# Mixture-of-experts stage of a two-layer transformer: from one tile per pipeline step to two

## The reference, cut to what matters

```python
z_norm = _rmsnorm(z, norm_w)
scores = softmax(z_norm @ router_w)                  # 8 experts
topk_vals, topk_idx = top_k(scores, 2)               # then divided by their sum
mixed = sum_e cw[:, e] * ((silu(z_norm @ w1[e]) * (z_norm @ w3[e])) @ w2[e])   # 128 -> 256 -> 128
z = z + mixed
```

## Time and profile before

| | us |
|---|---|
| median of 3 runs | 2763.26 |
| lowest, highest | 2757.63, 2775.57 |
| the profiled execution, its own time | 2753.16 |
| its span in the profile | 2751.4 |
| mean granted clock of TensorE over the span | 0.888 |
| expert tiles, first to last input transpose | 1600.8 to 2690.2 |

### The profile page before, as it was taken

The page is one execution under the profiler, slowest core; times in us unless marked ns, Lnnn a source line. Parts: engine busy times, 40 slices in busy tenths (PEclk is TensorE's granted clock), DMA queues, the critical chain, the costliest instruction groups (busy, mean ns, idle before and its releaser), DMA issues. The chain is left out here.

```text
span 2751.4 us, 46785 instructions
## 1 busy us (share of the span) xinstructions
PE 2116.8 (77%) x14679; PEld 1042.8 (38%) x14679; DVE 1843.9 (67%) x5385; ACT 1460.1 (53%) x3354; POOL 1225.6 (45%) x1710
## 2 busy tenths in 40 slices
PE   5999999999899899999999455674838575666762
PEld 1222222222256444444444234452526353444441
DVE  8999999999867788888888454453534344344324
ACT  1888888888833477777777322241414232333231
POOL 5433434342002477777775244335352524433434
PEclk9999999999999799999999777686968787777886
DMA  6535444353101233233332112222222222222322
GB/s 162 135 99 147 114 121 127 112 142 106 56 1 46 48 94 95 72 72 95 94 84 59 52 59 68 59 68 61 75 62 67 68 66 66 71 65 62 90 77 83
DMA packets 224609, 226.92 MB, mean 82 GB/s; under 512 B 34032, under 2 KB 187504, under 8 KB 224368
## 3 DMA queue, kind: packets, MB, share of 16 engines
q1 hardware_dynamic: 152432, 164.62, 22.5%
q0 software_dynamic: 16384, 33.59, 4.2%
q10 hardware_dynamic: 55552, 25.71, 3.2%
HBM read 96.48 MB, written 125.76 MB: 81 GB/s over the span
## 5 line engine op out<-in xcount | busy, mean ns | idle before, releaser
L702 ACT ACTIVATE mid_PT<-mid_ps 128x512 f32<-128x512 f32 (+2 forms) x1792 | 913.9, 568 | 258.2 <-PE mid_ps L583 250.3
L785 DVE TENSOR_REDUCE mid_nmax<-mid_ps 128x1 f32<-128x512 f32 (+2 forms) x1280 | 777.0, 658 | 61.7 <-PE mid_ps L562 36.8
L562 PE MATMUL mid_ps<-KT,QT 48*128 48x512 bf16 (+3 forms) x2048 | 605.0, 351 | 68.2 <-DVE mid_nmax L785 49.7
L1379 PE MATMUL moe_ps<-moe_w,moe_xinT 128*128 x638 | 398.4, 711 | 309.8 <-ACT moe_xinT L1434 159.0
L583 PE MATMUL mid_ps<-QT,KT 64*128 64x512 bf16 (+3 forms) x2048 | 562.5, 346 | 2.6 <-ACT mid_PT L702 2.2
L1528 DVE TENSOR_TENSOR moe_h<-moe_ps,moe_sg 128x256 f32<-128x256 f32 x319 | 135.1, 423 | 528.1 <-ACT moe_sg L1443 331.8
L599 PE MATMUL mid_ps<-mid_PT,vv 128*32 128x512 f32 (+3 forms) x4096 | 464.9, 527 | 16.2 <-POOL mid_PT L914 12.4
L1434 ACT ACTIVATE moe_xinT<-moe_ps,norm_w 128x128 f32<-128x128 f32 x319 | 117.0, 367 | 652.1 <-remote 349.7
L1490 POOL DMA_INDIRECT rows_in<-moe_xn,moe_scat_idx x256 | 248.4, 970 | 453.9 <-DVE moe_scat_idx L1676 380.1
L562 PEld LDWEIGHTS mid_ps<-KT,QT 48*128 48x128 bf16 x2048 | 159.0, 94 | 585.8 <-DVE mid_nmax L785 397.7
L1503 POOL DMA_INDIRECT moe_yg<-rows_out,moe_gat_idx x256 | 246.1, 961 | 241.3 <-issue 121.5
(11 more groups left out here) (260 smaller groups left out, 3028.3 us busy)
## 6 DMA issues: line engine op xcount, KB each, us to landing
l_spread<-mid_slots SPq DMA_DIRECT2D x128, 384.0 KB, 5.4
rows_in<-mid_blank SPq DMA_DIRECT2D x64, 512.0 KB, 3.7
QT<-l_spread SPq DMA_DIRECT2D x128, 192.0 KB, 4.4
KT<-l_spread SPq DMA_DIRECT2D x128, 192.0 KB, 5.2
moe_xin<-rows_in SPq DMA_DIRECT2D x319, 64.0 KB
rows_out<-moe_y ACTq DMA_DIRECT2D x319, 64.0 KB
x<-in_L_attn_x_dram SPq DMA_DIRECT2D x8, 512.0 KB, 6.3
QT<-mid_mrows SPq DMA_DIRECT2D x256, 6.0 KB
```

Of the source, the lines that this page charges most:

```text
L562: mm = pe.matmul(ps[:, bank, n_keys * a:n_keys * (a + 1)], QT[rows, par, pair, i * P:(i + 1) * P], KT[rows, par, pair, 0:n_keys], start=Tr ...
L702: act.activation(weights_of(r, i, heads), ps[:, ring(S2, n - 2, k), 0:widths[i] * len(heads)], ACT.Exp, scale=scale).then_inc(exp_done, 1)
L785: dve.tensor_reduce(to, of, X_AXIS, ALU.max, negate=True).then_inc(s1_used, 1)
L1379: mm = pe.matmul(ps[:, GU[v % BANKS], :], xinT[:, v % 2, :], w13[:, bass.ds(expert(v), 1), :].rearrange("p a f -> p (a f)"), start=True, s ...
```

## The change

Tiles go in pairs through the same pipeline. A unit gets one tile more, so that its count is even. TensorE does each of its four kinds of work for the two tiles of a pair and signals once; ScalarE copies both inputs in one instruction (128x256), both transposed h in one (128x512) and does one silu for both (128x512 from two banks); VectorE has one product and one copy per pair, and one store carries both results. Ages are now 2, 4 and 6 pairs. The ring is 4 pairs. PSUM: two pairs of banks for gate/up, one bank for the transposed h of a pair, two banks that each hold a pair's inputs and results, and one bank for the side transposes, the router and the counts together. So there are new waits: the h transposes wait for the copy of the pair before (`h_copied`), the side transposes for the last step of the group before (`scat_ready`), the result copy for the input copy out of the same bank (`x_copied`). The order on TensorE in a step is now: result, gate/up, h, input. Side steps run behind pairs, TensorE's one pair later, and `begin` and `transfers` are written anew.

```diff
-    RING, HELD = 8, 8
-    TURN, MULT, LAG = 6, 2, 8
-    BANKS = 3
+    RING, HELD = 4, 12
+    MULT, TURN, LAG = 2, 4, 6
...
-    tiles_in = [2 * IT * n + EXPERTS - 1 for n in sizes]
+    tiles_in = [2 * IT * n + EXPERTS for n in sizes]
     base_of = [sum(tiles_in[:u]) for u in range(UNITS + 1)]
     N = base_of[UNITS]
+    PAIRS = N // 2
...
-    begin = {2: 0, 3: 14, 4: 29, 5: 47, 6: 63, 7: 78, 8: 95, 9: 115, 10: 135, 11: 157, 12: 179, 13: 201, 14: 223, 15: 246,
-             16: 270, 17: 283, 18: 292, 19: 314, 20: 325}
-    transfers = ("s0 s1 s2 s3 g8 s4 s5 g9 s6 g10 s7 g11 s8 g12 s9 g13 s10 g14 s11 s12 g15 s13 g16 s14 g17 g18 s15 "
+    begin = {2: 0, 3: 15, 4: 31, 5: 49, 6: 63, 7: 81, 8: 97, 9: 120, 10: 141, 11: 163, 12: 183, 13: 205, 14: 225, 15: 251,
+             16: 281, 17: 301, 18: 309, 19: 319, 20: 333}
+    transfers = ("s0 s1 s2 s3 s4 g8 s5 g9 s6 s7 g10 g11 s8 s9 g12 s10 g13 g14 s11 s12 g15 g16 s13 s14 g17 g18 s15 "
                  "g19 g20 g21 g22 g23").split()
...
 
-        return 16 * sum(1 for n in range(base_of[u + 1]) if n % RING == s)
+        return 16 * sum(1 for p in range(base_of[u + 1] // 2) if p % RING == s)
...
-        GU, XHY, T, R = (0, 1, 2), (3, 4, 5), 6, 7
-        X, H, Y = 0, P, P + FF
-        psR = ps[:, R, 0:IT * EXPERTS].rearrange("p (t e) -> p t e", e=EXPERTS)
-        psK = ps[:, R, IT * EXPERTS:(2 * IT + 1) * EXPERTS].rearrange("p (t e) -> p t e", e=EXPERTS)
+        GU, H, XY, S = (0, 2), 4, (5, 6), 7
+        X, Y = 0, 2 * P
+        psR = ps[:, S, 0:IT * EXPERTS].rearrange("p (t e) -> p t e", e=EXPERTS)
+        psK = ps[:, S, IT * EXPERTS:(2 * IT + 1) * EXPERTS].rearrange("p (t e) -> p t e", e=EXPERTS)
...
+        xin = sb("xin", [P, RING, 2, DIM], F32)
+        xinT = sb("xinT", [P, 2, 2 * P], F32)
+        sg = sb("sg", [P, 2, 2, FF], F32)
+        h = sb("h", [P, 2, 2, FF], F32)
+        hT = sb("hT", [P, 2, 2 * FF], F32)
+        y = sb("y", [P, RING, 2, DIM], F32)
...
-        def run(tile, side, behind):
+        def run(duo, side, behind):
 
             for k in range(EARLY):
                 for s in range(STAGES):
                     side(k, s)
-            for n in range(N + LAG + 1 + behind):
-                tile(n)
-                for k, s in sides(n - behind):
-                    side(k, s)
+            for p in range(PAIRS + LAG + 1 + behind):
+                duo(p)
+                for n in range(2 * (p - behind), 2 * (p - behind) + 2):
+                    for k, s in sides(n):
+                        side(k, s)
...
-                row = sp.value_load(row_of[0:1, n:n + 1], min_val=0, max_val=EXPERTS * CAP - P)
-                if n >= RING:
-                    sp.wait_ge(step_done, n - RING + 1)
-                sp.dma_start(xin[:, n % RING, :], rows_in[u % CHUNKS][bass.ds(row, P), :]).then_inc(x_loaded[n % RING], 16)
+                for j in range(2):
+                    n = 2 * p + j
+                    row = sp.value_load(row_of[0:1, n:n + 1], min_val=0, max_val=EXPERTS * CAP - P)
+                    if j == 0 and p >= RING:
+                        sp.wait_ge(step_done, p - RING + 1)
+                    sp.dma_start(xin[:, p % RING, j, :], rows_in[u % CHUNKS][bass.ds(row, P), :])\
+                      .then_inc(x_loaded[p % RING], 16)
...
-            def tile(n):
-                if n == 0:
+            def duo(p):
...
+                bank = XY[p % 2]
+                if is_pair(p - 2):
+                    pe.wait_ge(x_copied, p - 1)
+                if is_pair(p - 2 - LAG):
+                    pe.wait_ge(y_ready, p - 2 - LAG + 1)
+                v = p - LAG
+                if is_pair(v):
+                    pe.wait_ge(h_copied, v + 1)
+                    for j in range(2):
+                        e = expert(2 * v + j)
+                        for c in range(FF // P):
+                            mm = pe.matmul(ps[:, bank, Y + j * DIM:Y + (j + 1) * DIM],
+                                           hT[:, v % 2, j * FF + c * P:j * FF + (c + 1) * P],
+                                           w2[:, bass.ds(e, 1), c, :].rearrange("p a d -> p (a d)"),
+                                           start=(c == 0), stop=(c == FF // P - 1))
+                v = p - MULT
+                if is_pair(v):
                     pe.wait_ge(x_copied, v + 1)
-                    if v >= BANKS:
-                        pe.wait_ge(h_ready, v - BANKS + 1)
-                    mm = pe.matmul(ps[:, GU[v % BANKS], :], xinT[:, v % 2, :],
-                                   w13[:, bass.ds(expert(v), 1), :].rearrange("p a f -> p (a f)"), start=True, stop=True)
-                v = n - LAG
-                if is_tile(v):
-                    e = expert(v)
-                    pe.wait_ge(h_copied, v + 1)
-                    for c in range(FF // P):
-                        mm = pe.matmul(ps[:, bank, Y:Y + DIM], hT[:, v % 2, c * P:(c + 1) * P],
-                                       w2[:, bass.ds(e, 1), c, :].rearrange("p a d -> p (a d)"),
-                                       start=(c == 0), stop=(c == FF // P - 1))
-                if is_tile(n):
-                    pe.wait_ge(x_loaded[n % RING], 16 * (n // RING + 1))
-                    mm = pe.transpose(ps[:, bank, X:X + P], xin[:, n % RING, :], w["ident"][:, :])
-                    pe.reg_load(held[n % HELD], expert_of[0:1, n:n + 1])
-                if n < N + LAG:
+                    if v >= 2:
+                        pe.wait_ge(h_ready, v - 1)
+                    for j in range(2):
+                        mm = pe.matmul(ps[:, GU[v % 2] + j, :], xinT[:, v % 2, j * P:(j + 1) * P],
+                                       w13[:, bass.ds(expert(2 * v + j), 1), :].rearrange("p a f -> p (a f)"),
+                                       start=True, stop=True)
+                v = p - TURN
+                if is_pair(v):
+                    pe.wait_ge(h_ready, v + 1)
+                    if v >= 1:
+                        pe.wait_ge(h_copied, v)
+                    for j in range(2):
+                        for c in range(FF // P):
+                            mm = pe.transpose(ps[:, H, j * FF + c * P:j * FF + (c + 1) * P],
+                                              h[:, v % 2, j, c * P:(c + 1) * P], w["ident"][:, :])
+                if is_pair(p):
+                    pe.wait_ge(x_loaded[p % RING], 32 * (p // RING + 1))
+                    for j in range(2):
+                        mm = pe.transpose(ps[:, bank, X + j * P:X + (j + 1) * P], xin[:, p % RING, j, :], w["ident"][:, :])
+                        pe.reg_load(held[(2 * p + j) % HELD], expert_of[0:1, 2 * p + j:2 * p + j + 1])
+                if p < PAIRS + LAG:
                     mm.then_inc(step_done, 1)
...
@@ -1402,15 +1415,15 @@
                         pe.wait_ge(added, k - GROUPS + 1)
                     else:
                         pe.wait_ge(z_ready, k + 1)
-                    if k + a >= 1:
-                        pe.wait_ge(t_used, 2 * k + a)
+                    if a == 1:
+                        pe.wait_ge(t_used, 2 * k + 1)
+                    elif k >= 1:
+                        pe.wait_ge(scat_ready, k)
                     for t in range(4):
-                        mm = pe.transpose(ps[:, T, t * P:(t + 1) * P], z[:, tiles_of(k) + 4 * a + t, :], w["ident"][:, :])
+                        mm = pe.transpose(ps[:, S, t * P:(t + 1) * P], z[:, tiles_of(k) + 4 * a + t, :], w["ident"][:, :])
                     mm.then_inc(t_made, 1)
                 if s == 8:
                     pe.wait_ge(t_used, 2 * k + 2)
-                    if k >= 1:
-                        pe.wait_ge(scat_ready, k)
...
-            run(tile, side, 2)
+            run(duo, side, 1)
...
+            def duo(p):
+                if p < PAIRS + LAG:
+                    act.wait_ge(step_done, p + 1)
+                if is_pair(p):
+                    act.activation(xinT[:, p % 2, :], ps[:, XY[p % 2], X:X + 2 * P], ACT.Copy, scale=w["norm_w"][:, 0:1])\
                        .then_inc(x_copied, 1)
-                v = n - TURN
-                if is_tile(v):
-                    act.activation(hT[:, v % 2, :], ps[:, XHY[n % BANKS], H:H + FF], ACT.Copy).then_inc(h_copied, 1)
-                v = n - MULT
-                if is_tile(v):
-                    if v >= BANKS:
-                        act.wait_ge(h_ready, v - BANKS + 1)
-                    act.activation(sg[:, v % BANKS, :], ps[:, GU[v % BANKS], 0:FF], ACT.Silu).then_inc(sg_ready, 1)
-                v = n - LAG - 1
-                if is_tile(v):
+                v = p - MULT
+                if is_pair(v):
+                    if v >= 2:
+                        act.wait_ge(h_ready, v - 1)
+                    act.activation(sg[:, v % 2, :, :], ps[:, GU[v % 2]:GU[v % 2] + 2, 0:FF], ACT.Silu).then_inc(sg_ready, 1)
+                v = p - TURN
+                if is_pair(v):
+                    act.activation(hT[:, v % 2, :], ps[:, H, :], ACT.Copy).then_inc(h_copied, 1)
```

(27 more changed lines are left out.)

45 lines of the change are left out of this document (10 added, 35 removed).

## The result

The pair kernel takes 2796.08 us (median of 4 runs, 2792.77 to 2798.28) beside 2760.45 for the one before (median of 4): ratio 1.0114, 95% interval [1.0092, 1.0135]. The forecast was 2713 us, faster; the measured value is the one of the rival in which a batch lets a fixed amount of work pass (2797), but the terms that make it up are largely others, as the last part shows. The profiled execution took 2795.2 us, span 2793.5, clock 0.884.

What follows compares the result with a forecast made beforehand. The prediction saw TensorE held by late signals during GpSimd's batches of indirect DMAs. Its terms, +21 - 80 + 13 - 4 = -50 us, took the 2763.3 us median to 2713 us; 8-in-10 range 2615 to 2790.

Steps and rivals of the forecast that it cites:

- a batch lets a fixed amount of work pass: Rival: windows over GpSimd's batches still pass 5 or 6 tiles, the change only adds tiles and waits: +34, 2797 us; chance 0.24.
- Item 1: Tiles: 8 spare tiles per unit instead of 7, nine more empty tiles at 2.33 us: +21 us (bounds 15 and 44).
- Item 2: In the batches: 1.5 more tiles pass per window, 23 windows at 2.33 us a tile: -80 us (bounds 0 and -204).
- Item 4: Places and waits: the single h bank's and VectorE's new waits stay hidden: 0 to +0.8 us a pair.
- the head start of 4 tiles: In a batch, TensorE gets 4 tiles instead of 2 beyond the last signal, less about one: +1 tile per window.
- a slow rhythm of 12.3 us per pair: In a stalled batch, a pair takes 12.3 us, 6.15 per tile instead of 7.8: +0.6 tile per window.
- Item 3: Instructions merged on ScalarE and VectorE: shorter per pair, but beside a busy TensorE, so 0 saved on the path.
- the two signs of being wrong: Signs of "wrong altogether": TensorE under 90% busy between batches, or batches moved so that more stand back to back.
- Item 5: Routing steps 5 and 6 fall into the same pair for 12 of 14 groups, 1.05 us each: +13 us (bounds 0, 36.4).
- The new starts and the new order at 0, with +-15.: Routing steps' new start numbers and the new order of transfers: put at 0, with +-15 us.
- Item 6: The tail behind the last input transpose: 6 pair drain steps instead of 8 steps: -4 us (bounds -10 and +5).

Runs made afterwards that it cites:

- a_gu_h2: Pair kernel with two banks for h, gate and up of both tiles sharing one bank (first tile computed with the second's): 2769.59 us, ratio 1.0019.

## Why the prediction was wrong

Where the time goes was seen rightly: into late signals in the batches, not into TensorE's own work. How many steps get through a batch was seen wrongly. Step by step:

**Item 1, +21.** 15.5 measured, within its bounds (15 and 44), the four batches that joined by it included.

**Item 2, -80: the step that failed.** "TensorE may still run two steps beyond the last signal, but a step is now two tiles". It may not. Item 4 looked at the single h bank only for the time between batches. The wait for `h_copied` of the pair before is a wait for the signal of the step before, and in a batch that is the late one. So the head start of 4 tiles was that of one pair and two thirds of the next, and a window passes 5.7 tiles, not 7.3. The second term of the item, a slow rhythm of 12.3 us per pair, failed as well: it was a line through two points, 7.79 us from one window and 5.3 from the drain, and the copies come 7 to 43 us apart. Put back, the second step ahead is worth 27.4 us, and not 80: with two h banks a window holds 7.1 tiles by its input transposes (135 in 19 windows; 113 with one bank), but only 0.6 tile more by its matmuls, and the joined batches have no second share. In the earlier trace rows the prediction read 41 as the lower end of the matmuls in a single batch; it is 33 (1644.1 to 1666.7).

"A batch lets a fixed amount of work pass" was given 0.24 and has come out in its main claim, that the change brings nothing per window, with two corrections: the amount is that of a window, however many batches it holds, and it does grow a little with the steps ahead. That its 2797 us is the measured time is luck: its +34 were 21 for tiles and 13 for side waits. Measured are 15.5 for the tiles, nothing for the side waits in this kernel, and about 14 for the order of the transfers, which it had at 0. Nor do the single changes add up: tiles 15.5, h bank 27.4 and order 14 make 57 where the pair kernel is 36 slower.

**Item 3, 0.** Right, and the sizes too: product 0.690 us (0.7 taken), ScalarE per pair 0.474 + 0.591 + 0.599 = 1.66 us (1.76 taken).

**Item 4, 0 to 0.8 us a pair.** Right between the batches (7.4 us in all where nothing is held), wrong in them, see item 2. Of the two signs of being wrong that the prediction named, one is batches that stand back to back more often, and these it got. The other, TensorE under 90% busy between batches (88%), is met only by the cut of the windows, as shown above.

**Item 5, +13.** In the pair kernel the idle time before the side transposes is unchanged (35.8). The collision is real, but hidden behind the h bank, and where a batch stands over it, it isn't 1.05 us but 14 (in a_gu_h2).

**"The new starts and the new order at 0, with +-15."** At the upper end: the order alone is 14 us, and 11 instead of 6 batches are joined, 9 with the old order. The prediction had counted 29 batches in 23 windows and then averaged over the windows, without asking what a joined batch costs more than a single one.

**Item 6, -4.** +15 by the profiled execution: g22 starts right behind g21, and under it the last pairs stand until 2740. But another execution of the same kernel parts loop and tail otherwise (a tail of 54.2 us, 7 less than before), so the size of this term stays open. Moving g22 away brings 5.6 us.

In what the forecast left out, a tile between batches takes 2.17 us instead of 2.30. With the batches apart pairs are 24 us faster than single tiles (2738.0 to 2714.08). No run tells what makes these 24 us.

## What to carry to other kernels

Before counting how many steps an engine may run ahead, follow every wait of the step back to the signal that it hangs on; one buffer that lost its twins shortens the whole pipeline, though its wait is hidden in the quiet stretches. Where a disturbance has a fixed price per stretch, look first at how many stretches there are and which join: 3.1 us of pause between two batches passed six tiles more, and keeping batches apart took 28 us off one kernel and 82 off the other, where the edits of the pipeline were worth 9 to 29. And time a schedule on more than one chip before tuning it against a stall: here the version that is 2% faster with the stall is, but for two gathers, 1.4 to 1.6% slower without.

## What the runs showed of the hardware that was not expected

- One and the same kernel has medians of 2760 to 2766 us in four sets of runs, on at least three chips, and 2302 on another, in two sets of 13 and 7 runs, within 0.4%. The difference is the lateness of TensorE's signals while GpSimd issues indirect DMAs: from 4 to 40 us in the pair kernel on the one, none on the other, with the DMAs themselves unchanged at 0.96 to 0.97 us each. What differs between the chips no run shows. The Trainium skill ("SBUF — State Buffer", "SBUF: two separate sides") has engine ports and DMA ports that cannot contend; the other chip, where the same transfers hold nothing, agrees with it, and the road by which a signal gets late elsewhere stays open.
- Where signals are late, back-to-back batches pass hardly more than the first alone (a mean of 51, 61.5 and 63 matmuls for one, two and three), and 3.1 us without an indirect DMA are enough for a whole share again (115).
- Product of 128x512 on VectorE: 0.690 us, where 128x256 took 0.423; ScalarE's silu and copy of 128x512: 0.59 and 0.60, with 0.39 and 0.38 for 128x256.
